# One spectral transformer tower kernel: middle and last stage in one block, first stage with kept orders

## What is computed

```
# tokenizer: x is (64 blocks, 256 degrees l, 257 orders m, re/im)
coeff = complex(x) * sqrt_eig                      # scale of each (l, m)
s = einsum('nlm,mlk->nkm', coeff, pct)             # per order m: Legendre sum over l
h = irfft(s, n=512)                                # (64, 256 rows, 512)
# attention
z = layernorm(h)
logits = tanh((z @ K) @ z.T + bias); band of 12 around the diagonal; softmax
h = h + softmax @ z
# feed-forward: only rows with marks x0 >= 0.5 and x1 >= 0.5 change
z = layernorm(h); a, b nibbles = argmax(z[64:80] > .5), ..., op = z[29]
y = 7 layers of 160 x 160 with relu on (nibbles, op)
out = h + z;  out[128:144] += 2*one_hot(round(y...)), out[144:160] likewise
```

## Time and profile before

| | us |
|---|---|
| median of 3 runs | 1486.73 (1485.23 to 1488.94) |
| the profiled execution | 1486.39, span 1484.3 |
| stage 1 | 0 to 349 |
| stage 2, SP's first DMA / PE's last attention product | 355.8 / 1258 |
| stage 3 | 1274.5 to 1484.3 |
| a step of stage 3 | 35.2 |
| PE, DVE, ACT, POOL busy (share of the span) | 91%, 63%, 61%, 37% |
| mean granted PE clock | 0.963 |

### The profile page before, as it was taken

The page is one execution under the profiler, slowest core; times in us unless marked ns, Lnnn a source line. Parts: engine busy times, 40 slices in busy tenths (PEclk is TensorE's granted clock), DMA queues, the critical chain, the costliest instruction groups (busy, mean ns, idle before and its releaser), DMA issues. The chain is left out here.

```text
span 1484.3 us, 30741 instructions
## 1 busy us (share of the span) xinstructions
PE 1346.7 (91%) x8813; PEld 1166.9 (79%) x8813; DVE 930.7 (63%) x2025; ACT 901.5 (61%) x1956; POOL 550.5 (37%) x1390
## 2 busy tenths in 40 slices
PE   4999787776899999999999999999999997599993
PEld 3577665665899999999999999999999997355551
DVE  1132222222678878887887887888788786477771
ACT  1223222222577777777777777777777776467772
POOL 0000000000055555555555555555555555102222
PEclk8999999997999999999999999999999999699997
DMA  9979999997333333333333333233333322000000
GB/s 362 419 279 424 422 422 422 423 422 245 90 82 95 97 81 82 97 83 80 96 82 81 94 89 80 88 96 82 79 96 82 82 67 51 24 6 9 8 4 4
DMA packets 87990, 219.97 MB, mean 148 GB/s; under 512 B 20676, under 2 KB 33616, under 8 KB 75408
## 3 DMA queue, kind: packets, MB, share of 16 engines
q1 hardware_dynamic: 77456, 184.43, 38.3%
q10 hardware_dynamic: 5120, 33.56, 5.6%
q0 software_dynamic: 5376, 1.52, 0.6%
HBM read 148.16 MB, written 73.07 MB: 149 GB/s over the span
## 5 line engine op out<-in xcount | busy, mean ns | idle before, releaser
L192 PE MATMUL s1b<-pg,cg 128*128 128x256 f32 x1024 | 247.2, 401 | 65.6 <-DVE cg L156 64.9
L460 PE MATMUL ps_k<-sphi,Glo 128*128 128x256 f32 x1024 | 292.2, 285 | 0.0
L459 PE MATMUL ps_k<-splo,Ghi 128*128 128x256 f32 x1024 | 290.9, 284 | 0.0
L192 PEld LDWEIGHTS s1b<-pg,cg 128*128 128x128 f32 x1024 | 202.2, 201 | 112.3 <-issue 58.0
L458 PE MATMUL ps_k<-sphi,Ghi 128*128 128x256 f32 x1024 | 288.6, 282 | 0.0
L156 DVE TENSOR_TENSOR cg<-xg,se 128x1024 f32<-128x1024 f32 x64 | 78.1, 1225 | 219.9 <-DMA pg<-in_pct_dram 184.8
L243 ACT COPY stage<-s1b 128x512 f32<-128x512 f32 x128 | 74.4, 587 | 230.1 <-PE s1b L192 212.0
L779 POOL TENSOR_SCALAR ve<-var 128x2 f32<-128x2 f32 x64 | 14.0, 218 | 526.5 <-ACT squares L627 526.4
L458 PEld LDWEIGHTS ps_k<-sphi,Ghi 128*128 128x128 f32 x1024 | 194.6, 190 | 2.4
L459 PEld LDWEIGHTS ps_k<-splo,Ghi 128*128 128x128 f32 x1024 | 193.0, 189 | 2.7
L460 PEld LDWEIGHTS ps_k<-sphi,Glo 128*128 128x128 f32 x1024 | 193.7, 189 | 0.0
(11 more groups left out here) (141 smaller groups left out, 3089.0 us busy)
## 6 DMA issues: line engine op xcount, KB each, us to landing
pg<-in_pct_dram SPq DMA_DIRECT2D x64, 1024.0 KB, 26.2
xg<-in_xs_dram SPq DMA_DIRECT2D x64, 512.0 KB, 25.2
spec<-stage ACTq DMA_DIRECT2D x64, 512.0 KB, 8.1
xt<-spec SPq DMA_DIRECT2D x64, 512.0 KB, 5.4
out_dram<-o SPq DMA_DIRECT2D x64, 512.0 KB, 2.8
rrow<-rs SPq DMA_DIRECT2D x64, 128.0 KB, 4.7
recs<-rec SPq DMA_DIRECT2D x16, 160.0 KB, 5.4
recs<-rec,idx POOLq DMA_INDIRECT x128, 2.3
```

What stands on the lines that cost most here:

```text
L192: last = nc.tensor.matmul(bank[(b % sets) * PARTS + part][:, m % 2, :], cg[:, b % SETS, m * 2 + h, :], pg[:, b, m * 2 + h, :], start=(h == ...
L459: nc.tensor.matmul(out_ap, whi, mlo, start=False, stop=False)
L460: last = nc.tensor.matmul(out_ap, wlo, mhi, start=False, stop=(j == n - 1))
```

## The change

Three parts. In stage 1, the eight side products are spread: one each after groups 3, 5, 7, 9 (K·FT) and 11, 13, 15, 17 (KF·FT), Glo after 14, 16, 18, 19; twenty groups instead of eight are written out, with three PSUM sets. The last twelve groups (HELD = 12, 48 orders, re and im) are not stored to `spec`: ACT copies them into an SBUF tensor `hold` that outlives the stage (the side matrices use the same bytes before). In stage 2, SP first loads blocks 0 to 3 with three DMAs each, 104 partitions from `spec` and twice 24 partitions from one partition of `hold`, and then stores the kept orders of blocks 4 to 63 from `hold` to `spec`; load(4) waits for these stores. Stages 2 and 3 are one block; tensors of stage 3 lie over `hold` and over tensors that the last slots no longer use, and use the same PSUM banks. The weights are copied and split at the head of slot 60, the records of step 0 are loaded in slot 63 behind the scatters of blocks 0 to 59, and its features, first layer and layer 1 run in slots 63 to 66. If these blocks filled fewer than 1024 places, later places are shifted up to 1024 (`shift`, `far`), so that step 0 never needs them.

```diff
+LEAD = 20
+HELD = 12
+FROM = P - HELD * GM // 2
+AHEAD = NB - 4
 # stage 1
+        KF_AFTER = {3: 0, 5: 1, 7: 2, 9: 3}
+        G_AFTER = {11: 0, 13: 1, 15: 2, 17: 3}
+        GLO_AFTER = {14: 0, 16: 1, 18: 2, 19: 3}
+        def groups(eng, group):
+            for g in range(LEAD):
+                group(g, g % RING1)
+            with eng.Fori(LEAD, GROUPS - HELD - RING1 + 1, RING1) as g0:
+                for u in range(RING1):
+                    group(g0 + u, (LEAD + u) % RING1)
+            for g in range(GROUPS - HELD, GROUPS):
+                group(g, g % RING1)
 # PE
+                if isinstance(g, int) and g == LEAD - 1:
+                    pe.wait_ge(dve_Glo, CH)
+                    pe.wait_ge(copied, LEAD * PARTS)
 # ACT
+                    if held:
+                        to = hold[:, (g - GROUPS + HELD) * GM + 2 * j:(g - GROUPS + HELD) * GM + 2 * j + 2, :]
+                    else:
+                        to = stage[:, half, row + 2 * j:row + 2 * j + 2, :]
+                    nc.scalar.copy(to, bank[at * PARTS + j][:, :, :]).then_inc(copied, 1)
-                if b % 2 == 1:
+                if b % 2 == 1 and not held:
...
-                act.wait_ge(stored[half], 32 * (GROUPS // 4))
+                act.wait_ge(stored[half], 32 * ((GROUPS - HELD) // 4))
 # stage 2, SP ahead of the slots
             for n in range(4):
-                load(n, n)
+                sp.dma_start(xt[0:FROM, n].rearrange("p (h q) w -> p h (q w)", h=2),
+                             spec[n].rearrange("(h p q) w -> p h (q w)", h=2, q=2)[0:FROM]).then_inc(x_loaded[n], 16)
+                for c in range(2):
+                    sp.dma_start(xt[FROM:P, n, 2 * c:2 * c + 2, :].rearrange("p q w -> p (q w)"),
+                                 const.hold[c * NB + n:c * NB + n + 1, :, :].rearrange("o (p q) w -> o p (q w)", q=2)
+                                 ).then_inc(x_loaded[n], 16)
+            for c in range(2):
+                sp.dma_start(spec[4:NB, (c + 1) * NLAT - HELD * GM:(c + 1) * NLAT, :],
+                             const.hold[c * NB + 4:c * NB + NB]).then_inc(hold_stored, 16)
             sp.wait_ge(const.rec_filled, 2)
...
 # SP, in the slots
                     sp.wait_ge(dve_splo, i + 1)
+                    if isinstance(i, int) and i == 0:
+                        sp.wait_ge(hold_stored, 32)
                     load(i + 4, k)
+                if isinstance(i, int) and i == AHEAD + 3:
+                    for r in range(4):
+                        sp.wait_ge(rec_sent[r], 32 * (AHEAD // 4))
+                    sp.wait_ge(rec_used, 1)
+                    load_records(0, 0)
 # PE, rank, and the end of the slots
+                if isinstance(n, int) and n >= NB - 2:
+                    pe.wait_ge(act_pos, n)
                 if has(i - 1):
                     probs_T(i - 1)
+                if has(i - 3) and not (ending and i == NB + 2):
                     rank(i - 3, (k + 1) % 4)
+                if ending and i == NB:
+                    pe.wait_ge(ffn_loaded, 16 * len(ffn_consts))
+                    pe.wait_ge(weight_lo, 4)
+                    features_T(0)
+                if ending and i == NB + 1:
+                    pe.wait_ge(dve_eo, 4 * NB)
+                    pe.wait_ge(dve_h2, 2 * NB)
+                    first_layer(0)
+                    layer(0, 1, lambda: rank(NB - 1, (NB - 1) % 4))   # rank behind the main tiles
+            slots(nc.tensor, slot)
+            pe.wait_ge(act_pos, NB)
+            steps(nc.tensor, body)
 # ACT, in the slots
+                if isinstance(i, int) and i == AHEAD:
+                    act.wait_ge(ffn_loaded, 16 * len(ffn_consts))
+                    act.wait_ge(hold_stored, 32)
+                    nc.scalar.copy(W1h[:, :, :], const.W1f[:, :, :]).then_inc(weight_hi, 1)
+                    nc.scalar.copy(Whi[:, :, :], const.Wf[:, :, :]).then_inc(weight_hi, 1)
...
+                if ending and i == NB:
+                    round_in(0)
+                if has(i - 3) and not (ending and i == NB + 2):
                     n = i - 3
...
+                if ending and i == NB + 1:
+                    relu(0, 0)
+                    n = NB - 1
+                    act.wait_ge(pe_rank, n + 1)
+                    act.wait_ge(pool_idx, (n - 1) * 3)
+                    nc.scalar.copy(pos[:, n % 2, :], ps_l[:, 0, 0:3]).then_inc(act_pos, 1)
                 if has(i - 2):
...
                         nc.scalar.activation(o[:, k % 2, t], h2[:, k % 2, t], ACT.Identity,
...
+            slots(nc.scalar, slot)
+            relu(0, 1)
+            steps(nc.scalar, body)
 # DVE, in the slots
+                if isinstance(i, int) and i == AHEAD:
+                    dve.wait_ge(hold_stored, 32)
+                    split_weights()
+                    nc.vector.memset(feat[:, :, :], 0.0).then_inc(start, 1)
+                    nc.vector.memset(res[:, :, :], 0.0).then_inc(rec_used, 1)
...
+                    if ending and i == NB + 1:
+                        split_tile(0, 0, 0)
                     for t in range(TILES):
                         nc.vector.tensor_scalar(x2[:, r2, t, :], h2[:, r2, t, 0:P], rstd2[:, r2, t:t + 1], None,
...
+                    if ending and i == NB + 1:
+                        for g in range(1, TILES5):
+                            split_tile(0, 0, g)
...
+                if isinstance(i, int) and i == NB - 1:
+                    dve.wait_ge(start, 1)
+                    features(0, 0)
+            slots(nc.vector, slot)
+            split(0, 1)
 # POOL, count and shift; the marks of blocks 62 and 63 are made one slot earlier
+                    if isinstance(n, int) and n == NB - 1:
+                        nc.gpsimd.tensor_tensor(total[:, :], pos[:, r2, 2:3], shift[:, :], ALU.add).then_inc(count_set, 1)
+                        pool.wait_ge(count_set, 1)
+                        settled(pool)
+                        nc.gpsimd.tensor_copy(const.count_i[:, :], total[:, :]).then_inc(count_set, 1)
 # every engine, behind its slots
-        def steps(eng, at_once, ahead, body, phases=1):
+        def steps(eng, body, phases=1):
+            eng.wait_ge(count_set, 2)
             count = eng.value_load(const.count_i[0:1, 0:1], min_val=0, max_val=NB * NLAT)
-            at_once()
-            with eng.If(count > 0):
-                ahead()
```

More of the change, by code:

```diff
@@ L161, in se_view, with group @@
                 return v.unsqueeze(2).to_broadcast([P, GM * 2, P])
+            def group(g, b):
+                if isinstance(g, int):
+                    dve.wait_ge(loaded[b], 32 * (g // RING1) + 32)
+                else:
+                    dve.wait_ge(loaded[b], g * (32 // RING1) + (32 - b * (32 // RING1)))
+                wait(dve, summed, (g - SETS + 1) * PARTS)
+                nc.vector.tensor_tensor(
+                    cg[:, b % SETS], xg[:, b], se_view(g), ALU.mult).then_inc(scaled, 1)
+                if isinstance(g, int) and g in GLO_AFTER:
+                    c = GLO_AFTER[g]
+                    dve.wait_ge(act_Ghi, c + 1)
+                    nc.vector.tensor_tensor(const.Glo[:, c], side(c), const.Ghi[:, c].bitcast(F32),
+                                            ALU.subtract).then_inc(dve_Glo, 1)
             dve.wait_ge(se_loaded, 16)
@@ L169, in _, with group @@
             nc.vector.memset(const.rec0[:, :, 0:1], FAR).then_inc(const.rec_filled, 1)
-            for b in range(RING1):
-                dve.wait_ge(loaded[b], 32)
-                scale(b, b, 3)
-                if b in (6, 7):
-                    for c in (2 * (b - 6), 2 * (b - 6) + 1):
-                        dve.wait_ge(act_Ghi, c + 1)
-                        nc.vector.tensor_tensor(const.Glo[:, c], side(c), const.Ghi[:, c].bitcast(F32),
-                                                ALU.subtract).then_inc(dve_Glo, 1)
-            with nc.vector.Fori(RING1, GROUPS - RING1 + 1, RING1) as g0:
-                for b in range(RING1):
-                    dve.wait_ge(loaded[b], g0 * (32 // RING1) + 32)
-                    scale(g0 + b, b)
+            groups(nc.vector, group)
         @block.tensor
         def _(pe):
-            def multiply(g, b, sets=SETS):
+            def group(g, b):
+                sets = 3 if isinstance(g, int) and g < LEAD else SETS
+                at = g % sets if isinstance(g, int) else b % SETS
                 pe.wait_ge(scaled, g + 1)
@@ L392, in stage2_blocks @@
         rec_sent = [sem(f"rec_sent{i}") for i in range(4)]
+        pool_shift = sem("pool_shift")
+        pool_rows = sem("pool_rows")
+        count_set = sem("count_set")
+        start = sem("ffn_start")
+        weight_hi = sem("weight_hi")
+        weight_lo = sem("weight_lo")
+        rec_loaded = [sem(f"rec_loaded{i}") for i in range(2)]
+        rec_used = sem("rec_used")
+        oc_free = sem("oc_free")
+        feat_part = sem("feat_part")
+        feat_made = sem("feat_made")
+        feat_T = sem("feat_T")
+        xin_made = sem("xin_made")
```

(47 more changed lines are left out.)

900 lines of the change are left out of this document (419 added, 481 removed).

## The result

The changed kernel takes 1482.59 us in the median of 20 runs (1476.51 to 1487.88), the kernel before, beside it, 1488.26 (1485.23 to 1493.81). The ratio is 0.9960, 95% interval 0.9947 to 0.9973: 4 to 8 us faster. 1476.4 was forecast, with a range of 1459 to 1490. In a second series of runs the ratio was 0.9949 (0.9933 to 0.9964), 1472.60 us against 1481.25. The first profiled run took 1485.50 us (span 1483.7), 2.9 above its median.

A forecast was written before the change was run, and what follows sets the result against it. Stage 1 was taken as bound by the DMA engines, stage 2 by PE, the seams by neither. Terms -12.7 - 12.4 - 4.9 + 30 + 7.5 - 17.5 = -10.0 took 1486.4 to 1476.4 us, range 1459 to 1490.

The forecast's parts named there:

- Part 1: Stage 1, 70 to 110 us: spreading the side products closes the hole in DMA rate, -12.7 us.
- Part 2: Stage 1's end: twelve groups kept save 12.4 us of stores and 4.9 us of waiting for the last store.
- the wait at the end: End of stage 1: no longer waiting for the last store saves 4.9 us, with 1.96 us left for ending a block.
- Part 3: Front of stage 2: stores of kept orders and added loads delay block 0's row transfers, +30 us (13.9 to 41.7).
- rival (a): Front of stage 2: kept-order stores run at 423 GB/s, so this costs +14 us; total 1460.4 us, chance 0.22.
- The one-partition reads: Front of stage 2: eight small DMAs fetching kept orders of blocks 0 to 3, +3 us (0 to 14.9).
- Rival (b): Front of stage 2: one-partition reads are slow, over 17.7 us in all; total 1503 us, chance 0.15.
- first in, first out: Front of stage 2: SP's queue runs in order, so block 0's row transfers stand behind the kept-order stores; within +30 us.
- Part 4: Slot 60: weight copies and splits make PE stand 5.6 us, and its low clock adds some 2 us; +7.5 us.
- Part 5: Drain of stage 2: the first step starts there, so layer 2 comes earlier, -17.5 us (-12 to -22).
- rival (c): Drain: ACT's order, the count load and low clock leave only -9 us; total 1484.9 us, chance 0.13.
- layer 0 and 1 run at the pace of before: Drain, step 0: these two layers keep their old pace, apart from +0.5 us for x2 between the splits.

The follow-up runs named there:

- e2_nohold: Changed kernel with the kept orders undone: all 64 groups stored in stage 1, blocks 0 to 3 loaded with one DMA each; 1461.97 us.
- e1_spread: Kernel before with only the side products of stage 1 spread over groups 3 to 17, no orders kept; 1473.98 us, ratio 0.9945.
- the last two kernels: Changed kernel with weights dealt out, drain moves, later blanks and constants: kept orders read directly from SBUF, 1431.40 us; no orders kept, 1445.88 us.
- three kernels: Changed kernel with kept-order stores on ACT's queue, 1472.56 us; also blanks and constants later, 1466.63 us; also stores about 12 us later, 1461.79 us.
- the second pair: Second profiles of both kernels, nothing edited: the profiled executions took 1486.81 us (kernel before) and 1472.56 us (changed kernel).

## Why the prediction was right

The direction, the range and the mechanism held: a gain of 30 us in stage 1 eaten by as much at the front of stage 2. Point by point:

- **Part 1** (-12.7): the spread kernel starts stage 2 11.4 us earlier, 10.3 up to the last load (342.04 to 331.71) and 1.1 behind it. About right. One profile fixes it to a few us only: e2_nohold, with the same spread products and all groups stored, starts stage 2 at 340.51, 3.9 us before e1_spread; its DMA engines move 425 GB/s from 110 to 300 us, the other's 422.
- **Part 2** (-17.3): 17.2 us between the last two kernels, but by two errors that cancel. The stores gave 10.4 where 12.4 were forecast, and the wait at the end 6.8 where 4.9 were: the forecast kept 1.96 us for the end of a block, and with no store to wait for this end takes 0.25.
- **Part 3** (+30): +32.6 and +32.3. Without stores lsc stands at +30.7, so the stores cost 59.1 - 30.7 = 28.4 us, where 26.8 were forecast at 220 GB/s; they moved 238. Taking the rate of the earlier trace rows's pair at 350 us was the right choice, and rival (a), 423 GB/s, falls. The one-partition reads were put at +3: block 0's input came 5.3 us after the first DMA instead of 3.9, and with the blanks behind them lsc is 4.1 us late. These are the issues of the reads, which were to hide because the queue is full: SP took 8.6 us for them at a DMA share of 0.70. So 28.4 and 4.1 make up the 32.6. Rival (b), small reads over 17.7 us, falls with them. By the port figure of the Trainium skill (SBUF — State Buffer, "Door 1: The DMA port swizzle") part 3 was to be 34 us; 32.6 lies between that and the forecast and does not tell them apart. The forecast's reason, first in, first out within SP's queue, was too narrow: three kernels show that the stores hold up other queues' transfers too, even 1 KB.
- **Part 4** (+7.5): the two gaps are the very ones named, but PE stood 3.5 and 2.9 us in them where 5.6 were forecast, since its products between them ran at the lower clock and so part of DVE's delay was spent working. The clock cost 2.8 and 1.9 us, where 2 were forecast: right in size. PE's slot was 6.5 and 5.0 us longer. The whole row is 6.4 and 4.1; in the second pair the first two slots of the stage gave another 0.9 us.
- **Part 5** (-17.5): -16.4 and -18.0, so rival (c) with its -9 falls, but partly by luck. The working missed that DVE waits for POOL's rstd of block 63 ahead of the first split ("layer 0 and 1 run at the pace of before"): layer 1 was 2.2 us late by it. relu of layer 1 started at +12.8 instead of +11.8, and the count did decide layer 2, as said. Some 2.5 us in the other direction came from the last attention products, which ran at the upper clock: the forecast put the transposes of the features into PE's idle as "nothing on the path" and kept the lower clock behind it in its middle case.
- **Not in the sum at all**: +1.6 us between the last scatter and the end of the program, in each kernel with merged stages (11.5 instead of 9.9 us behind POOL's last instruction), and waits in the steps in some executions, 6.5 us in the first profile.

The size was off: 5.7 and 8.7 us in the medians where 10 were forecast. The profiled pairs give 0.6 and 14.1, which brackets the medians: in the first the changed kernel's execution was 2.9 us above its median and the other 1.9 below, in the second the one of the kernel before was 5.9 above the 1480.96 of its own runs. Mis-sized to the bad side are the end, 1.6 us missing in the sum, and part 3 by 2.3 to 2.6; to the good side stage 1 by 1.3 to 3.5 and part 4 by 1.1 to 3.4. These errors are as large as what is left of the gain, so a sum near the measured time is in part luck. The median of 1482.59 lies nearer to rival (c)'s 1484.9 than to the forecast's 1476.4, but not for (c)'s reason. In the first series the rest would be the waits in the steps, if its other executions had them; only one was seen, so this is not shown.

## What to carry to other kernels

A byte taken off a bound stage is only saved if it does not come back ahead of a short transfer that something waits for; see what stands behind a large store on every queue, not only on its own. Read kept data where it is needed rather than write it out later: the same orders gained 14.5 us read in place and lost 11 to 15 when stored. A block of 4 us of DVE work in one piece made its slot 5.0 to 6.5 us longer, more than its length because PE's clock fell behind the gap; in pieces of up to 1.5 us it cost nothing.

## What was not expected of the hardware

- Two stores of 60 partitions x 48 KB keep the DMA engines' busy share at 1.01 and move 238 GB/s, 56% of the 423 of stage 1, and during them a 1 KB transfer on another queue took 28.4 us. One reads the lower half of the partitions, the other the upper, and the second lands 14 to 16 us behind the first.
- 120 reads of 48 KB from a single partition, spread over 60 slots, cost no time (slots of 13.76 us with and without them); beside the large stores a block's input, two such reads among it, came after 34.9 us.
- After the same idle of 2.67 us PE's next product took 0.77 us in one kernel (in both of its profiles, granted clock 0.50) and 0.47 in another with the same code there (granted clock 1.00).
- Every kernel with stages 2 and 3 in one block ends 1.6 to 1.7 us later behind POOL's last instruction. Why stays open.
